# Two attention layers and two expert layers on one core: the context stretch ordered anew by key tile

## The reference

```
x = x + softmax attention(layernorm(x), ctx)     16 query heads of 128, 4 key heads, RMS norm on queries and keys
x = x + experts(layernorm(x))
x = x + linear attention(layernorm(x), ctx, mask) 16 heads of 16, 64 features a head
x = x + experts(layernorm(x))

linear attention, the part that depends on ctx alone:
  k = heads(ctx @ Wk.T + bk);  v = heads(ctx @ Wv.T + bv)
  k' = relu(k @ Wkf.T) * mask
  kv = sum over rows of k' x v;   k_sum = sum over rows of k'

softmax attention, the queries:
  q = rms_norm(heads(layernorm(x) @ Wq)) / sqrt(128)
```

## Time and profile before

| | |
|---|---|
| Timed runs, median of 3 | 1410.51 us (1408.31 to 1410.95) |
| Profiled execution | 1409.69 us, of which the instructions span 1407.9 us |
| TensorE busy | 1237.1 us, 88% of the span |
| VectorE, ScalarE, GpSimd busy | 890.0, 739.2 and 539.0 us |
| Mean granted clock of TensorE | 0.943 of full speed |
| TensorE busy from 79.0 to 385.9 us (six batches) | 260.11 of 306.9 us |

### The profile page before, as it was taken

How to read it: one execution, slowest core, us unless ns; L and a number is a source line. 1 busy time by engine, 2 the same in 40 slices (tenths; PEclk the granted TensorE clock), 3 DMA queues, 4 the chain that set the end, 5 groups by cost and what they waited for, 6 DMA issues and landing times. The chain is left out here.

```text
span 1407.9 us, 27107 instructions
## 1 busy us (share of the span) xinstructions
PE 1237.1 (88%) x9559; PEld 1059.3 (75%) x9559; DVE 890.0 (63%) x1859; ACT 739.2 (53%) x1262; POOL 539.0 (38%) x560
## 2 busy tenths in 40 slices
PE   5888888888886999999999999999999767978697
PEld 4777777777773888888888888888888656855585
DVE  4654455455454778787888887787886494442543
ACT  3544545444453666657666665766756323431542
POOL 1422222222223635465353545536363061512452
PEclk9999999999997999999999999999999877987799
DMA  4111101101003111101111110111000050005000
GB/s 144 39 31 50 39 15 51 37 19 47 8 2 88 44 45 44 46 3 41 44 44 44 33 54 0 44 44 44 0 0 1 29 199 1 1 0 205 1 0 14
DMA packets 38748, 56.05 MB, mean 40 GB/s; under 512 B 3058, under 2 KB 37154, under 8 KB 38178
## 3 DMA queue, kind: packets, MB, share of 16 engines
q1 hardware_dynamic: 38226, 54.82, 12.2%
q10 hardware_dynamic: 464, 0.46, 0.1%
HBM read 54.81 MB, written 0.46 MB: 39 GB/s over the span
## 5 line engine op out<-in xcount | busy, mean ns | idle before, releaser
L1094 POOL TENSOR_TENSOR att_sq<-att_work,att_sq 128x500 fp32r<-128x500 f32 x96 | 127.1, 1324 | 180.9 <-DVE att_sq L992 180.9
L1099 POOL TENSOR_TENSOR att_k<-att_work,att_k 128x500 fp32r<-128x500 f32 x96 | 129.7, 1351 | 159.5 <-DVE att_k L1000 159.5
L101 PE MATMUL att_csum<-att_pT,att_cn 125*128 125x448 f32 x384 | 155.0, 404 | 1.4 <-DVE att_pT L1038 0.4
L544 DVE SCALAR_TENSOR_TENSOR kvs_ks<-kvs_keys_ps,kvs_bk,kvs_ks 64x500 fp32r<-64x500 f32 x96 | 70.8, 738 | 134.6 <-ACT kvs_ks L456 133.0
L352 PE MATMUL kvs_feat<-kvs_f,kvs_ks 128*125 128x256 f32 x768 | 117.6, 291 | 31.6 <-DVE kvs_kp L599 15.9
L916 ACT ACTIVATE att_pr<-att_pr,att_nmx 112x1500 f32<-112x1500 f32 (+1 forms) x96 | 108.6, 1131 | 67.6 <-DVE att_nmx L1029 67.6
L103 PE MATMUL att_csum<-att_pT,att_cn 125*128 125x448 f32 x384 | 140.1, 365 | 0.0
L102 PE MATMUL att_csum<-att_pT,att_cn 125*128 125x448 f32 x384 | 139.3, 363 | 0.0
L456 ACT ACTIVATE kvs_ks<-kvs_keys_ps,kvs_bk 64x500 fp32r<-64x500 f32 x96 | 64.9, 676 | 140.5 <-PE kvs_keys_ps L103 139.1
L1038 DVE TENSOR_TENSOR att_pT<-att_ring,att_pT 125x448 fp32r<-125x448 f32 x192 | 118.4, 617 | 22.6 <-ACT att_pT L932 22.4
L352 PEld LDWEIGHTS kvs_feat<-kvs_f,kvs_ks 128*125 128x125 f32 x768 | 101.4, 190 | 40.3 <-issue 28.5
(11 more groups left out here) (254 smaller groups left out, 3316.5 us busy)
## 6 DMA issues: line engine op xcount, KB each, us to landing
attention_raw_t<-in_ctxT SPq DMA_DIRECT2D x45, 500.0 KB, 4.1
att_raw_n<-in_ctx SPq DMA_DIRECT2D x16, 750.0 KB
w_gate<-in_gate SPq DMA_DIRECT2D x1, 2112.0 KB, 9.8
w_up<-in_up SPq DMA_DIRECT2D x1, 2112.0 KB, 14.6
kvs_raw_q<-in_wq SPq DMA_DIRECT2D x8, 256.0 KB, 2.8
wo_raw<-in_wo SPq DMA_DIRECT2D x4, 512.0 KB, 6.6
w_down<-in_down SPq DMA_DIRECT2D x1, 2048.0 KB, 18.3
w_gate<-in_gate SPq DMA_DIRECT2D x1, 1760.0 KB, 13.4
```

The costliest lines, as they stand in the source:

```text
L101: nc.tensor.matmul(out, w_lo, x_hi, start=start, stop=False, skip_group_check=True)
L544: nc.vector.scalar_tensor_tensor(ks[64:128, c, 2 * m + h, :], keys_ps[y, 0:CH], bk[y, m:m + 1], ks[0:64, c, 2 * m + h, :].bitcast(F32), AL ...
L1094: nc.gpsimd.tensor_tensor(sq[1][:, i % 2, :], work[:, i % 2, :], sq[0][:, i % 2, :].bitcast(F32), ALU.subtract).then_inc(sq_lo, 1)
L1099: nc.gpsimd.tensor_tensor(k[1][x], work[:, i % 2, :], k[0][x].bitcast(F32), ALU.subtract).then_inc(k_lo, 1)
```

## The change

The work of the first phase is the same; the tiles at which its steps stand are others, in all four engines' `step`:

| | before | after |
|---|---|---|
| `split` of a context chunk | after a chunk's fourth tile (t = 3, 7, 11) | after its second (t = 1, 5, 9) |
| `add` on TensorE | t = 1, 4, 7, 10 | t = 2, 5, 8, 11 |
| `take_sums`, `turn`, `read_blocks` | t = 2, 2, 2 | t = 3, 4, 4 |
| `project` | t = 0, 6 (last batch 0, 3, 6, 9) | t = 4, 8 |
| `square`, split of the square | 1 tile later | 1 tile later |
| `mean_square` | 3 later (last batch 2) | 2 later |
| `root`, `normalise` | 4 later (last batch 2) | 3 later |
| heads in the batches | 0, then 2 in each of six, then 4 | 2 in each of eight |
| `split_heads` | t = 8 (last batch 4) | t = 1 |
| batch 0: `xn`, `turn_x`, evictions | t = 0 to 3, 4, 5 and 6 | all at 0, 1, 2 and 3 |
| batch 0: weights of the softmax attention | t = 9, 10 | t = 6, 10 |

`project` also waits for the bank `mean` to be free, since the transposes of x use both banks. The diff, with like pieces left out:

```diff
-        SQUARE_AT, MEAN_AT, ROOT_AT = 1, {False: 3, True: 2}, {False: 4, True: 2}
+        SQUARE_AT, MEAN_AT, ROOT_AT = 1, 2, 3
...
-        def queries_at(i, first, last, t, after):
-
-            if first:
-                return []
-            heads = {0: (0, 2 * (i - 1)), 6: (1, 2 * (i - 1) + 1)} if not last else \
-                {3 * n: (n % 2, NH - 4 + n) for n in range(4)}
-            return [heads[t - after]] if t - after in heads else []
+        def queries_at(i, t, after):
+
+            return [(n, 2 * i + n) for n in range(2) if t - after == 4 + 4 * n]
...
                 wait(pe, proj_free, h + 1)
+                wait(pe, mean_free, h + 1)
...
-                        if t % GROUP == 1:
-                            if t > 1:
+                        if t % GROUP == GROUP - 1:
+                            if t >= GROUP:
                                 add(i, t // GROUP - 1)
                             elif not first:
                                 add(i - 1, NG - 1)
                         if n in (0, 2) and to_project is not None:
                             keys(*to_project, n // 2)
-                        if t == 2 and not first:
+                        if t == 4 and not first:
                             turn(i - 1)
-                        if first and t == 4:
+                        if first and t == 1:
                             turn_x()
...
-                        if t == 2 and not first:
+                        if t == 3 and not first:
                             take_sums(i - 1)
...
+                        if n == 1 and to_split is not None:
+                            split(*to_split)
+                        if t == 1:
+                            split_heads(i)
...
-                        if not last and t == 8:
-                            split_heads(i)
-                        if last and t == 4:
-                            split_heads(i)
-                    if to_split is not None:
-                        split(*to_split)
...
-                        if t == 2 and not first:
+                        if t == 4 and not first:
                             read_blocks(i - 1)
...
-                        if first and t < TT:
-                            nc.vector.tensor_scalar(xn[:, t, :], x[:, t, :], mv[:, t, 0:1], rstd[:, t:t + 1],
-                                                    ALU.subtract, ALU.mult).then_inc(xn_done, 1)
...
+                            for y in range(TT):
+                                nc.vector.tensor_scalar(xn[:, y, :], x[:, y, :], mv[:, y, 0:1], rstd[:, y:y + 1],
+                                                        ALU.subtract, ALU.mult).then_inc(xn_done, 1)
```

More of the change, by code:

```diff
@@ L424, in step @@
                             keys(*to_project, n // 2)
-                        if t == 2 and not first:
+                        if t == 4 and not first:
                             turn(i - 1)
-                        if first and t == 4:
+                        if first and t == 1:
                             turn_x()
-                        for k, h in queries_at(i, first, last, t, MEAN_AT[last]):
+                        for k, h in queries_at(i, t, MEAN_AT):
                             mean_square(h, k)
-                        for k, h in queries_at(i, first, last, t, 0):
-                            project(h, k, i - 1 if not last else h // 2)
+                        for k, h in queries_at(i, t, 0):
+                            project(h, k, i)
             pe.wait_ge(w_lo, 2)
@@ L497, in step @@
                             keys(*to_project, n // 2)
[L498 removed]
+                        for k, h in queries_at(i, t, SQUARE_AT):
                             square(h, k)
[L500 removed]
+                        for k, h in queries_at(i, t, ROOT_AT):
                             root(h, k)
[L502 to L504 removed]
+                        if n == 1 and to_split is not None:
+                            split(*to_split)
+                        if t == 1:
+                            split_heads(i)
+                        if first and t in (2, 3):
+                            act.wait_ge(turned_done, t - 1)
+                            nc.scalar.activation(xnT[0][:, t - 2, :], (proj, mean)[t - 2][:, 0:NTOK], ACT.Copy)\
                                 .then_inc(x_hi, 1)
[L506 removed]
+                        if first and t in (6, 10):
                             act.wait_ge(a_loaded, 32)
[L508 to L514 removed]
+                            w = t // 10
+                            nc.scalar.activation((wk0, wv0)[w][0][:], raw_a[:, w], ACT.Copy).then_inc(a_hi, 1)
             nc.scalar.dma_start(x[:], a["x"].rearrange("(t p) d -> p t d", p=TP)).then_inc(x_loaded, 16)
@@ L602, in step @@
                             keys(*to_project, n // 2)
-                        if t == 2 and not first:
+                        if t == 4 and not first:
                             read_blocks(i - 1)
-                        for k, h in queries_at(i, first, last, t, SQUARE_AT):
+                        for k, h in queries_at(i, t, SQUARE_AT):
                             round_square(h, k)
-                        for k, h in queries_at(i, first, last, t, ROOT_AT[last]):
+                        for k, h in queries_at(i, t, ROOT_AT):
                             normalise(h, k)
@@ L680, in step @@
                                                 zeros[:], ALU.add).then_inc(v_mask, 1)
-                        for k, h in queries_at(i, first, last, t, SQUARE_AT):
+                        for k, h in queries_at(i, t, SQUARE_AT):
                             split_square(h, k)
-                        if first and t in (9, 10):
-                            w = (wk0, wv0)[t - 9]
-                            pool.wait_ge(a_hi, t - 8)
-                            nc.gpsimd.tensor_tensor(w[1][:], raw_a[:, t - 9], w[0][:].bitcast(F32),
-                                                    ALU.subtract).then_inc(a_lo, 1)
-                        if not last and t == 8:
-                            split_heads(i)
-                        if last and t == 4:
-                            split_heads(i)
-                    if to_split is not None:
-                        split(*to_split)
+                        if n == 1 and to_split is not None:
+                            split(*to_split)
+                        if t == 1:
+                            split_heads(i)
+                        if first and t in (6, 10):
+                            w = t // 10
+                            pool.wait_ge(a_hi, w + 1)
+                            nc.gpsimd.tensor_tensor((wk0, wv0)[w][1][:], raw_a[:, w], (wk0, wv0)[w][0][:].bitcast(F32),
+                                                    ALU.subtract).then_inc(a_lo, 1)
             nc.gpsimd.memset(fmap[:], 0.0).then_inc(fmap_set, 1)
```

12 lines of the change are left out of this document (6 added, 6 removed).

## The result

The changed kernel takes 1349.89 us (median of 4 runs, 1348.75 to 1350.85), the kernel before 1410.73 us (1408.31 to 1411.24). The ratio is 0.957, with a 95% interval of 0.956 to 0.959. The forecast was 1348 with a range of 1337 to 1368. The profiled span fell from 1407.9 to 1346.9 us, the mean granted clock rose from 0.943 to 0.959.

A forecast was written before the change was run, and what follows sets the result against it. TensorE's instructions plus its waits, decided by instruction order, were taken as the bound. Middle batches -54.5, first loop batch's tiles 0 to 2 -8.0, last batch -3.5, first +3.5: -62.5 from 1409.69, forecast 1348 us, range 1337 to 1368.

The forecast's parts named there:

- Pool's waits go, nothing takes their place: Keys on TensorE: splits two tiles earlier remove 15 waits for Pool, 22.3 us, and their refills.
- The relu waits: TensorE's waits for Vector's relu: 0.85 us each behind keys of tiles 0 and 2, 0.45 behind tile 6's.
- A new wait of sums at tile 5: Sums on TensorE wait for Vector's block reading, which follows tile 4's keys: 0.8 us a batch.
- Work 38.4 a batch: TensorE's instructions in one middle batch at full clock, added from start to start: 38.4 us.
- The clock, 0.7 a batch: Middle batches: time lost to TensorE's lower clock falls from 3.6 to 0.7 us a batch, ends 0 and 3.6.
- First batch, +3.5: Batch 0: two queries +3.3, transposes waiting for normalisations of x +2.8, less waits 1.5 + 1.1; ends 0 and +7.5.
- Last batch, -3.5: Rest of the last batch: 37.6 us before, 34.1 after, from work 30.6, waits and 0.3 of clock.
- A: Rival: TensorE's clock falls as often as before, +19, 1367 us; chance 0.14.
- B: Rival: only Pool's and the copy's waits go; relu waits return elsewhere, 31.0 us, clock's 3.6 kept; 1383; chance 0.10.
- C: Rival: slower, Scalar's early split waits for its chunk's load, up to 4.1 us per split, 1434; chance 0.03.
- D: Rival: no change at all, something unseen giving all back, 1410 us; chance 0.03.

The follow-up runs named there:

- e1: Kernel before with only the context splits moved to a chunk's second tile; 1374.67 us, ratio to before 0.974.
- e3: Changed kernel with the turn on TensorE and the block reading on Vector ahead of tile 4's keys; 1342.69 us, ratio 0.953.
- e6: Changed kernel with Vector's relu ahead of its masking of the values in odd tiles; 1343.39 us, ratio 0.953.
- e8: Changed kernel with the edits of e3, e4 and e6 together; 1328.07 us, ratio to before 0.943.
- e4: Changed kernel with the sharpening of rstd and the four normalisations of x ahead of tile 0's keys on Vector in batch 0; 1343.04 us, ratio 0.953.
- e7: Changed kernel with all four steps of head 0 one tile earlier (tiles 3, 4, 5, 6) in batches 1 to 7; 1366.55 us, ratio 0.970.
- e9: Changed kernel with only project and square of head 0 one tile earlier (tiles 3, 4) in batches 1 to 7; 1356.20 us, ratio 0.962.
- e11: Kernel of e3 with all four steps of head 0 one tile earlier in batches 1 to 7; 1358.26 us, ratio 0.965.

## Why the prediction was right, and where its sizes were off

1. *Pool's waits go, nothing takes their place.* Shown: the loop has none left, and e1 has this effect by itself. The lead of two tiles and a set of keys was enough in every batch.
2. *The relu waits: 0.85 after the keys of tiles 0 and 2, 0.45 after those of 6, none after 4.* Right in place and size: the idle in the rows is 0.61, 0.60 and 0.30, and with a refill of about 0.25 that is 0.86, 0.85 and 0.55. (The refill is an estimate from rows: the four matmuls ahead of such a wait take 0.71 us, where eight without a wait take 0.94 from start to start. For the sums at tile 5 it is no more than e3's 0.91 less 0.85.) e6 shows that Vector's order behind the keys makes them.
3. *A new wait of sums at tile 5, 0.8.* Measured 0.85, and e3 got 0.91 a batch back.
4. *Work 38.4 a batch.* e8 bounds it: 39.5 with hardly any waits. Work and waits together came to 41.35 in the forecast and 41.54 in the trace.
5. *The clock, 0.7 a batch.* Measured nothing: 1.00 over five batches. With the 0.2 that work and waits came out longer, the middle was 3.1 us better than forecast, 0.5 in each batch.
6. *First batch, +3.5: mis-sized, +6.1.* The queries' 3.3 were right (in the rows from start to start 1.22 and 0.41, twice). The wait of the transposes was taken as 2.8 within 2 to 4.3 and was 4.8, since Pool caught the normalisations with two instructions in a row, the context's split and that of the query weights, of which I had counted one; and it was the first normalisation that the split caught, not the last. The waits that went were 1.9 (3.5 before, 1.6 after beside the transposes') in place of 2.6. 3.3 + 4.8 - 1.9 = 6.2, which is in part luck, for a term is missing in it, the clock. It fell behind the transposes' wait (granted 0.66 from 30 to 40 us): the features of tile 2 took 1.52 us (row at 36.18) where such a row takes 1.10 at the full clock. By the starts of the rows, transposes, values and features at the lower level cost 2.3 us more, and a slow stretch of the kernel before at 26 to 29 us had cost 1.5 (both estimates); smaller items, not worked out, make up the difference. It fits with e4, which got 6.9 us back for a wait of 4.8. The Trainium skill, SBUF — State Buffer, section "SBUF: two separate sides", says that Vector and GpSimd share ports which one instruction holds until it ends; e4 and the kernel after agree, with 1.38 and 4.40 us for the same work. (By the recorded starts Vector's first was 0.05 us ahead of Pool's split and was held all the same.)
7. *Last batch, -3.5: mis-sized, -0.7.* Its waits came where they were forecast (0.53 at tile 4, 0.76 at tile 5, 0.29 at tile 8, 0.89 for the last square), 2.5 us in place of 3.2. Busy time was 31.8 in place of 30.6, in part the refills, and the 0.3 for the clock were not needed (1.00). Missing in the sum were the idle times marked "issue", 2.6 us. What makes them was not tried and stays open; the last batch is written out behind the loop and not inside it, and e3 and e8 have one of 1.4 to 1.5 us there too.

The errors were +2.6, +2.8 and -3.1 (and +0.2 and -1.1 in stretches that were given nothing), so that the total of -61.0 against -62.5 is closer than its terms: the mechanism of the loop was right, the closeness of the total is luck. Of the rivals, A (the clock keeps falling) is refuted by the 1.00 for this order; but e7, e9 and e11 show that it was a real one, with a wait of 2.06 us or a pair of 1.04 and 0.60. B needed relu waits of 31 us; there were 11.9. C needed Scalar's splits to wait for their loads: in the middle batches the only waits of TensorE are the four shown, and none goes back to a load; Scalar itself waited there (70 to 340 us) for TensorE alone. D is refuted by the interval.

## What to carry to other kernels

Edits that each remove a stall need not add up: an order laid for early splits makes a late split worse than the old order did (45.1 us of waits for 22.3). Price edits together, and try each alone to see which depends on which. An engine's place for an operation is good or bad by what stands behind it there, so a step moved by one tile (a root behind keys, a mean with no keys ahead of it) can cost more than the wait that it removes. Then look at each remaining wait for an operation ahead of the releasing one which nobody needs yet; three such swaps gave another 1.6% here.

## What the hardware showed that I had not expected

- One Vector instruction on four numbers a partition, with both operands in SBUF, took 1.24 us beside Pool's split and 0.16 to 0.17 otherwise. In the same trace two Vector instructions that read PSUM, at 32.49 and 33.43 us beside the split at 31.76, took their usual 0.48 and 0.69. So in these rows it goes by the operands' memory whether Pool holds Vector, and not by the size of the work; no run varied the one without the other.
- TensorE kept its higher level (2.4 GHz, granted 1.00) through five batches with single waits of up to 0.85 us. With a wait of 2.06, or with 1.04 and 0.60 close together, it fell to the lower one (1.2 GHz) in some batches and not in others, though their waits were alike: the same 96 matmuls then took 2.25 or 2.76 us in place of 1.53. In the kernel after it fell in none of the loop's batches, in e9 in three of six, in e11 in two. The Trainium skill, TensorE: Matmul & The Clock Gate, section "HAM oscillation — how this bites in real kernels", describes a loop whose clock falls in every round; its waits, for loads, are longer than any in the loops of these three kernels, so that no run here tests it.
- TensorE stood 1.0 and 1.4 us in the last batch, released by no engine, where the profile of before showed no such idle time in its last batch.
